# Sums of the dispatch weights by one product with a stationary of ones and a wide reciprocal, in an attention and soft-MoE kernel

## The reference

```python
x = layernorm(x, norm_g, norm_b)                       # B, 512, 256
logits = einsum('bnd,esd->bnes', x, se)                # 512 tokens x 1024 slots an image
dispatch = softmax(logits, axis=1)                     # over the tokens
combine = softmax(logits.reshape(B, N, -1), axis=-1)   # over the slots
slots = einsum('bnd,bnes->besd', x, dispatch)          # weighted sums of the tokens
```

## Time and profile before

| | us |
|---|---|
| median of 3 runs | 1199.85 (1196.84 to 1200.65) |
| the profiled execution, whole | 1196.4 |
| its span, first to last instruction | 1194.7 |
| TensorE busy | 1140.9 (96%) |
| VectorE, ScalarE, GpSimd busy | 780.1, 662.9, 579.2 |
| mean granted TensorE clock | 0.986 |

### The profile page before, as it was taken

The page is one execution under the profiler, slowest core; times in us unless marked ns, Lnnn a source line. Parts: engine busy times, 40 slices in busy tenths (PEclk is TensorE's granted clock), DMA queues, the critical chain, the costliest instruction groups (busy, mean ns, idle before and its releaser), DMA issues.

```text
span 1194.7 us, 19111 instructions
## 1 busy us (share of the span) xinstructions
PE 1140.9 (96%) x6849; PEld 897.2 (75%) x6882; DVE 780.1 (65%) x1251; ACT 662.9 (55%) x946; POOL 579.2 (48%) x399
## 2 busy tenths in 40 slices
PE   7799999999999999988999999979999999999996
PEld 5566667676666666656788888858888888888885
DVE  6878787979797978766677777644455454523344
ACT  2555466565656565656797777755555555530112
POOL 5555555555555556522666666664444544430000
PEclk9899999999999999999899999999999999999998
DMA  5645544645565454631144335365555445365661
GB/s 152 143 106 130 123 115 103 159 113 152 125 155 131 115 157 92 180 98 54 40 160 161 125 125 186 108 195 185 166 183 184 140 157 165 114 216 166 244 224 53
DMA packets 126670, 170.29 MB, mean 143 GB/s; under 512 B 47041, under 2 KB 77186, under 8 KB 126594
## 3 DMA queue, kind: packets, MB, share of 16 engines
q1 hardware_dynamic: 124018, 167.95, 48.2%
q10 hardware_dynamic: 2576, 1.35, 0.5%
HBM read 72.26 MB, written 37.75 MB: 92 GB/s over the span
## 4 chain that ended last, share of the span: by engine, by line
PE 79%; ACT 8%; DVE 6%; issue 3%; POOL 1%; ACTq 1%; DMA 1%; SPq 1%; another core or an unknown queue 0%; DVEq 0%; POOLq 0%
PE ring L455 11%; PE ring L456 11%; PE ring L457 11%; PE ring L1626 7%; PE tail L1487 6%; PE ring L1476 5%; PE ring L1460 4%; PE tail L455 4%; PE tail L456 4%; PE tail L457 4%; ACT pt L873 2%; PE ring L1509 2%; PE tail L1626 2%; PE ring L1563 2%; ACT x L892 2%
## 5 line engine op out<-in xcount | busy, mean ns | idle before, releaser
L1170 DVE TENSOR_REDUCE mx<-ring 128x4 f32<-128x512 f32 (+2 forms) x192 | 199.4, 1041 | 71.9 <-PE ring L1463 54.3
L873 ACT ACTIVATE pt<-ring 128x1024 f32<-128x1024 f32 (+1 forms) x192 | 167.4, 882 | 87.3 <-PE ring L1476 87.1
L723 POOL TENSOR_SCALAR_AFFINE_SELECT pt<-pt 128x512 f32<-128x512 f32 x128 | 81.7, 638 | 192.9 <-ACT pt L873 192.9
L1476 PE MATMUL ring<-qks 98*128 98x256 f32 (+3 forms) x512 | 136.7, 370 | 3.9 <-DVE mx L1170 1.9
L1460 PE MATMUL ring<-qks 96*128 96x384 f32 (+3 forms) x512 | 118.7, 334 | 9.0 <-DMA qks<-stg 3.5
L740 POOL TENSOR_TENSOR dl<-e,dh 128x1024 fp32r<-128x1024 f32 x32 | 76.5, 2404 | 93.4 <-ACT e L944 93.4
L764 POOL TENSOR_TENSOR hl<-hid,hh 128x512 fp32r<-128x512 f32 x64 | 82.7, 1302 | 77.1 <-ACT hh L979 77.1
L817 ACT ACTIVATE lat<-ring,blat 128x512 f32<-128x512 f32 x64 | 40.6, 685 | 128.3 <-PE ring L457 117.4
L1476 PEld LDWEIGHTS ring<-qks 98*128 98x128 f32 x512 | 79.0, 190 | 37.0 <-issue 20.1
L1288 DVE SCALAR_TENSOR_TENSOR hid<-ring,bias_e,gate 128x512 f32<-128x512 f32 x64 | 47.8, 747 | 80.9 <-ACT gate L973 47.0
L1460 PEld LDWEIGHTS ring<-qks 96*128 96x128 f32 x512 | 78.5, 192 | 29.5 <-ACT pt L873 18.8
(11 more groups left out here) (246 smaller groups left out, 3050.9 us busy)
## 6 DMA issues: line engine op xcount, KB each, us to landing
qks<-stg SPq DMA_DIRECT2D x378, 128.0 KB, 2.4
c_dram<-c2s SPq DMA_DIRECT2D x32, 512.0 KB, 5.0
c<-c_dram SPq DMA_DIRECT2D x32, 512.0 KB, 6.2
sl_dram<-sls SPq DMA_DIRECT2D x32, 256.0 KB, 3.4
wg<-in_wg SPq DMA_DIRECT2D x16, 512.0 KB, 5.3
wu<-in_wu SPq DMA_DIRECT2D x16, 512.0 KB, 6.0
wd<-in_wd SPq DMA_DIRECT2D x16, 512.0 KB, 6.9
sl<-sl_dram SPq DMA_DIRECT2D x16, 512.0 KB, 4.5
```

Of the source, the lines that this page charges most:

```text
L723: nc.gpsimd.affine_select(out=m, in_=m, compare_op=ALU.is_ge, fill=0.0, base=0, pattern=[[0, GH], [1, P]], channel_multiplier=-1).then_inc ...
L873: nc.scalar.activation(pt[j][:, h:h + heads, 0:n], heads_of(tile, heads, n), ACT.Exp, scale=SCALE).then_inc(empty, 1)
L1170: nc.vector.tensor_reduce(out=mx[:, g, h:h + heads, i], in_=heads_of(tile, heads, (i + 1) * P), axis=AX.X, op=ALU.max).then_inc(empty, 1)
L1476: last = nc.tensor.matmul(scores[:, h, :], qks[0:KS_ROWS + 2, g, 1, h0 + h, j * P:(j + 1) * P], qks[0:KS_ROWS + 2, g, 0, h0 + h, j * P:T], ...
```

## The change

The two steps `sumT` and `sumB` of a half become one, `sumB`, at the place of `sumT` in the lists of TensorE and VectorE. TensorE makes one f32 product with a stationary operand of 128x128 ones (a column of ones, broadcast) and the 512 columns of partial sums: each partition gets all 512 sums. VectorE takes the reciprocal of 128x512 out of PSUM straight to `sls[h][:, 1, :]`. The transposes, the small reduction and reciprocal, and ScalarE's copy are gone, with their buffers; a period has 15 fills. The column of ones is one more memset on GpSimd and 32 bytes among the constants, so all later arrays lie 32 bytes further; the counts of the start's semaphore move by one.

```diff
 PE_FRONT = (
-    ("sumT", -1, 1), ("topT", 0), ("c2", 0, 0), ("zT", 1), ("c2", 0, 1), ("topB", 0), ("sumB", -1, 1), ("slots", -1, 1), ("s1", 1, 0),
-    ("c2", 0, 2), ("c2", 0, 3), ("s1", 1, 1), ("sumT", 0, 0), ("s1", 1, 2), ("s1", 1, 3), ("sumB", 0, 0), ("slots", 0, 0),
+    ("sumB", -1, 1), ("topT", 0), ("c2", 0, 0), ("zT", 1), ("c2", 0, 1), ("topB", 0), ("slots", -1, 1), ("s1", 1, 0),
+    ("c2", 0, 2), ("c2", 0, 3), ("s1", 1, 1), ("sumB", 0, 0), ("s1", 1, 2), ("s1", 1, 3), ("slots", 0, 0),
 )
 DVE_FRONT = (
-    ("sumT", -1, 1), ("topT", 0), ("zT", 1), ("sub", 0, 0), ("sub", 0, 1), ("xn", 1), ("sub", 0, 2), ("sub", 0, 3), ("slots", -1, 1),
-    ("s1", 1, 0), ("s1", 1, 1), ("sumT", 0, 0), ("s1", 1, 2), ("s1", 1, 3), ("rows", 1), ("slots", 0, 0),
+    ("sumB", -1, 1), ("topT", 0), ("zT", 1), ("sub", 0, 0), ("sub", 0, 1), ("xn", 1), ("sub", 0, 2), ("sub", 0, 3), ("slots", -1, 1),
+    ("s1", 1, 0), ("s1", 1, 1), ("sumB", 0, 0), ("s1", 1, 2), ("s1", 1, 3), ("rows", 1), ("slots", 0, 0),
 )
 PE_LAST = (
-    ("topT", 0), ("c2", 0, 0), ("sumT", -1, 1), ("topB", 0), ("sumB", -1, 1), ("slots", -1, 1), ("c2", 0, 1), ("slots", 0, 0),
-    ("sumT", 0, 0), ("sumB", 0, 0), ("c2", 0, 2), ("c2", 0, 3), ("slots", 0, 1), ("sumT", 0, 1), ("sumB", 0, 1),
+    ("topT", 0), ("c2", 0, 0), ("sumB", -1, 1), ("topB", 0), ("slots", -1, 1), ("c2", 0, 1), ("slots", 0, 0),
+    ("sumB", 0, 0), ("c2", 0, 2), ("c2", 0, 3), ("slots", 0, 1), ("sumB", 0, 1), 
 )
...
+    one = place("one", [P, 1], f32)
...
+            nc.gpsimd.memset(one[:, :], 1.0).then_inc(pool_ready, 1)
...
-                elif name == "sumT":
-                    n = slice(st[2] * 4, st[2] * 4 + 4)
+                elif name == "sumB":
+                    h = st[2]
                     dve.wait_ge(full, fill_count(st))
-                    blink(nc.vector.tensor_reduce(out=es[:, n], in_=tile[:, 0, :].rearrange("p (j q) -> p j q", q=P), axis=AX.X, op=ALU.add))
-                    nc.vector.reciprocal(res[:, n], es[:, n]).then_inc(empty, 1)
+                    dve.wait_ge(sl_stored[h], b * NC * 16)
+                    if b == 0:
+                        read = ("cproj", B - 1)
+                        dve.wait_ge(pair_filled[slot(read)], fill_count(read))
+                    nc.vector.reciprocal(sls[h][:, 1, :], tile[:, 0, :]).then_inc(empty, 1)
...
-                elif name == "sumT":
+                elif name == "sumB":
                     h = st[2]
                     pe.wait_ge(summed, 4 * b + 2 * h + 2)
-                    for j in range(4):
-                        last = nc.tensor.transpose(tile[:, 0, j * P:(j + 1) * P], e2[2 * h][:, 0, j * P:(j + 1) * P], ident[:, :])
-                    last.then_inc(full, 1)
-                elif name == "sumB":
-                    h = st[2]
-                    src = ("sumT", b, h)
-                    pe.wait_ge(pair_drained[slot(src)], fill_count(src))
-                    for j in range(4):
-                        last = nc.tensor.transpose(tile[:, 0, j * P:(j + 1) * P], bcast(res[:, 4 * h + j:4 * h + j + 1], [P, P]), ident[:, :])
-                    last.then_inc(full, 1)
+                    nc.tensor.matmul(tile[:, 0, :], bcast(one[:, 0:1], [P, P]), e2[2 * h][:, 0, :], start=True, stop=True).then_inc(full, 1)
```

More of the change, by code:

```diff
@@ L114 @@
 PE_FRONT = (
-    ("sumT", -1, 1), ("topT", 0), ("c2", 0, 0), ("zT", 1), ("c2", 0, 1), ("topB", 0), ("sumB", -1, 1), ("slots", -1, 1), ("s1", 1, 0),
-    ("c2", 0, 2), ("c2", 0, 3), ("s1", 1, 1), ("sumT", 0, 0), ("s1", 1, 2), ("s1", 1, 3), ("sumB", 0, 0), ("slots", 0, 0),
+    ("sumB", -1, 1), ("topT", 0), ("c2", 0, 0), ("zT", 1), ("c2", 0, 1), ("topB", 0), ("slots", -1, 1), ("s1", 1, 0),
+    ("c2", 0, 2), ("c2", 0, 3), ("s1", 1, 1), ("sumB", 0, 0), ("s1", 1, 2), ("s1", 1, 3), ("slots", 0, 0),
 )
 ACT_FRONT = (
-    ("c2", 0, 0), ("c2", 0, 1), ("xn", 1), ("e", 0, 0), ("e", 0, 1), ("sumB", -1, 1), ("zh", 1), ("e", 0, 2), ("c2", 0, 2), ("s1", 1, 0),
-    ("c2", 0, 3), ("e", 0, 3), ("s1", 1, 1), ("s1", 1, 2), ("s1", 1, 3), ("sumB", 0, 0),
+    ("c2", 0, 0), ("c2", 0, 1), ("xn", 1), ("e", 0, 0), ("e", 0, 1), ("zh", 1), ("e", 0, 2), ("c2", 0, 2), ("s1", 1, 0),
+    ("c2", 0, 3), ("e", 0, 3), ("s1", 1, 1), ("s1", 1, 2), ("s1", 1, 3),
 )
 DVE_FRONT = (
-    ("sumT", -1, 1), ("topT", 0), ("zT", 1), ("sub", 0, 0), ("sub", 0, 1), ("xn", 1), ("sub", 0, 2), ("sub", 0, 3), ("slots", -1, 1),
-    ("s1", 1, 0), ("s1", 1, 1), ("sumT", 0, 0), ("s1", 1, 2), ("s1", 1, 3), ("rows", 1), ("slots", 0, 0),
+    ("sumB", -1, 1), ("topT", 0), ("zT", 1), ("sub", 0, 0), ("sub", 0, 1), ("xn", 1), ("sub", 0, 2), ("sub", 0, 3), ("slots", -1, 1),
+    ("s1", 1, 0), ("s1", 1, 1), ("sumB", 0, 0), ("s1", 1, 2), ("s1", 1, 3), ("rows", 1), ("slots", 0, 0),
 )
@@ L131 @@
 PE_LAST = (
-    ("topT", 0), ("c2", 0, 0), ("sumT", -1, 1), ("topB", 0), ("sumB", -1, 1), ("slots", -1, 1), ("c2", 0, 1), ("slots", 0, 0),
-    ("sumT", 0, 0), ("sumB", 0, 0), ("c2", 0, 2), ("c2", 0, 3), ("slots", 0, 1), ("sumT", 0, 1), ("sumB", 0, 1),
+    ("topT", 0), ("c2", 0, 0), ("sumB", -1, 1), ("topB", 0), ("slots", -1, 1), ("c2", 0, 1), ("slots", 0, 0),
+    ("sumB", 0, 0), ("c2", 0, 2), ("c2", 0, 3), ("slots", 0, 1), ("sumB", 0, 1),
 )
 ACT_LAST = (
-    ("c2", 0, 0), ("e", 0, 0), ("e", 0, 1), ("sumB", -1, 1), ("e", 0, 2), ("c2", 0, 1), ("e", 0, 3), ("weight", 0, 1), ("sumB", 0, 0),
-    ("weight", 0, 2), ("c2", 0, 2), ("weight", 0, 3), ("c2", 0, 3), ("sumB", 0, 1), ("weight", 0, 0),
+    ("c2", 0, 0), ("e", 0, 0), ("e", 0, 1), ("e", 0, 2), ("c2", 0, 1), ("e", 0, 3), ("weight", 0, 1),
+    ("weight", 0, 2), ("c2", 0, 2), ("weight", 0, 3), ("c2", 0, 3), ("weight", 0, 0),
 )
 DVE_LAST = (
-    ("topT", 0), ("sumT", -1, 1), ("sub", 0, 0), ("sub", 0, 1), ("sub", 0, 2), ("sub", 0, 3), ("slots", -1, 1), ("sumT", 0, 0),
-    ("slots", 0, 0), ("weight", 0, 1), ("weight", 0, 3), ("sumT", 0, 1), ("slots", 0, 1), ("weight", 0, 0),
+    ("topT", 0), ("sumB", -1, 1), ("sub", 0, 0), ("sub", 0, 1), ("sub", 0, 2), ("sub", 0, 3), ("slots", -1, 1), ("sumB", 0, 0),
+    ("slots", 0, 0), ("weight", 0, 1), ("weight", 0, 3), ("sumB", 0, 1), ("slots", 0, 1), ("weight", 0, 0),
 )
@@ L153 @@
 POOL_JOIN = ()
-PAIR_STEPS = ("lat", "max", "exp", "v", "yTT", "cproj", "wv", "seT", "zT", "s1", "topT", "topB", "sumT", "sumB", "c2", "slots")
+PAIR_STEPS = ("lat", "max", "exp", "v", "yTT", "cproj", "wv", "seT", "zT", "s1", "topT", "topB", "sumB", "c2", "slots")
 MISC_STEPS = ("wqk", "neg", "yT")
@@ L247, in block_kernel @@
     m2 = place("m2", [P, NS], f32)
-    es = place("es", [P, NS], f32)
-    res = place("res", [P, NS], f32)
     identb = place("identb", [P, P], bf16)
@@ L427, in block_kernel @@
     SE_DVE = WV_DVE + 2 + 3 * NEWTON + 1
-    MASK_READY, POOL_SETUP = 8, 10
+    MASK_READY, POOL_SETUP = 9, 11
     IN_LAT, IN_SMALL, IN_ROPE, IN_SG, IN_SE, IN_TAIL = 5, 7, 2, 3, 1, 4
     ATTN_CHAIN, COMBINE_CHAIN = G + G + 3 + 1 + 3 * NEWTON, 13
-    CHAIN = B * ATTN_CHAIN + B * 2
+    CHAIN = B * ATTN_CHAIN
     cos2, sin2 = (bcast(t[:, :].unsqueeze(1), [P, 2, T]) for t in (cos, sin))
@@ L669, in _ @@
             nc.gpsimd.memset(zeros[:, :, :], 0.0).then_inc(pool_ready, 1)
-            pool.wait_ge(pool_ready, 5)
+            nc.gpsimd.memset(one[:, :], 1.0).then_inc(pool_ready, 1)
+            pool.wait_ge(pool_ready, 6)
             for m in (ident, identb):
@@ L679, in _ @@
             nc.gpsimd.memset(va[:, :, :, HD:L], 1.0).then_inc(pool_ready, 1)
-            pool.wait_ge(pool_ready, 9)
+            pool.wait_ge(pool_ready, MASK_READY + 1)
             nc.gpsimd.memset(fp(qks[KS_ROWS:KS_ROWS + 2, :, 1, :, :]), 1.0).then_inc(pool_ready, 1)
@@ L1257, in _ @@
                     elif u % 2 == 0:
-                        read = ("sumT", b - 1, h)
+                        read = ("sumB", b - 1, h)
                         dve.wait_ge(pair_filled[slot(read)], fill_count(read))
```

2 lines of the change are left out of this document (removed).

## The result

| | before | after |
|---|---|---|
| median | 1198.34 us (4 runs) | 1226.23 us (4 runs, 1225.87 to 1230.95) |
| profiled execution, whole / span | 1196.4 / 1194.7 us | 1225.87 / 1224.1 us |
| mean granted TensorE clock | 0.986 | 0.977 |
| first front sum to first expert product (TensorE starts) | 804.14 - 578.98 = 225.2 us | 833.19 - 578.16 = 255.0 us |

The changed kernel takes 1.0236 times as long (95% interval 1.0218 to 1.0255), 28 us more. The last row holds all of it: the front has become 29.9 us longer, what lies before and after it has moved by less than 1 us.

The account below looks back on a forecast made before the run. TensorE's gapless queue of products bounds the periods, a chain of waits the end; 12.7 us over six periods plus 3.3 in the last image make 16.0 on the shown median 1199.85, so 1216 us, range 1205 to 1233.

Parts of the forecast that it names:

- The loop: Six front periods: two wide reciprocals on the chain between VectorE, ScalarE and TensorE, 29.77 to 31.9 us each, 12.7 in all.
- clock rival: New TensorE stops in each period lower its granted clock: 14.4 us more over six periods, 1230 us; chance 0.12.
- R: Time one wide reciprocal holds VectorE: forecast 3.03 us, 2.1 more than the reduction and small reciprocal it replaces.
- 25.84 + 2R: Front period's length, summed as 12.16 + 13.68 + 2R: 31.9 us forecast, against 29.77 before.
- The reciprocal's length: VectorE's reciprocal over 128x512 out of PSUM: 158 ns plus 512 elements at 5.75 ns, 3.10 us.
- this case's end: Upper end of the forecast case: reciprocal at 6.3 ns an element, R 3.3 us, sum 20.5 us, up to 1220.
- The last image: End of the front, where waits are exposed: reciprocals on the chain to the expert stage add 3.3 us.
- a sign that it was wrong: TensorE's granted clock below 1.00 between 590 and 780 us would show the forecast wrong.
- My stop of 1.6 us: TensorE stands still 1.6 us each period before c2 1, whose PSUM pair the reciprocal frees at 17.0 us.
- TensorE: no gain: Each of 16 sums swaps eight transposes, 0.87 us, for one f32 product, 0.86 us: nothing gained.
- the 32 bytes: Arrays behind the constants move by 32 bytes: taken at nothing, no row bearing on it.
- The fast divide: Rival: wide reciprocal at the copies' rate, R 0.62 us, 3.7 us gained in the last image, 1196; chance 0.12.

Follow-up runs that it names:

- e4_fill: Changed kernel with unused bf16 products filling TensorE's new stops (8 before c2 1, 15 and 12 before the last slots steps): ratio 1.0196 to before.
- e8_fill_apply: Changed kernel with TensorE's new stops filled by unused products and ScalarE's last apply step back at its old place: ratio 1.0156 to before.
- e10_copy_apply: Changed kernel with a copy for the wide reciprocal (division left out) and ScalarE's last apply step back at its old place: ratio 0.9974 to before.
- e3_apply: Changed kernel with ScalarE's last apply step, which had slid later in its list, back where the kernel before had it: ratio 1.0262 to before.
- e1_copy: Changed kernel with a 128x512 copy in place of the wide reciprocal, division left out: ratio 1.0001 to before.
- e7_pad: Kernel before with only the changed kernel's extra memset and 32 bytes among the constants: ratio 1.0000 to before.
- e2_half: Changed kernel with the reciprocal over 256 of 512 columns and a copy of the other 256: ratio 1.0079 to before.
- e11_lnexp2: Changed kernel's product, inverse by ScalarE's logarithm and exponential, logarithm alone freeing PSUM, sumB (b, 0) between s1 1 and s1 2 on ScalarE: ratio 0.9991 to before.

## Why the prediction was right, and where it was off

It said slower, by 16 us, by way of a loop; it is slower by 28, inside the range but nearer to its upper end. The loop is what the runs show; that the range held is in part luck, since of the 12 us beyond the forecast most come from a clock rival given 0.12 and from a step that the forecast did not have. The runs take the front's 29.9 us apart:

| step | front | part |
|---|---|---|
| changed kernel to e4_fill: clock held | 255.0 to 247.4 | 7.6 |
| e4_fill to e8_fill_apply: moved step put back | 247.4 to 244.7 | 2.7 |
| e8_fill_apply to e10_copy_apply: reciprocal to copy, stops gone | 244.7 to 223.0 | 21.7 |
| e10_copy_apply to before: all else that the change does | 223.0 to 225.2 | -2.1 |

The first two steps are one edit each, the third is two. The parts depend on the order in which they are taken: put back by itself, the moved step changed nothing (e3_apply, 255.1), as the clock fell once more. And e10_copy_apply has a fall of the clock of its own in the last image.

- **The loop** was right in every link: the stop before c2 1, topT behind the reciprocal, the drain of slots turned from TensorE's wait to ScalarE's, two reciprocals a period. With the measured reciprocal (R = 3.28 us; the next starts 717.33 - 714.07 = 3.26 after it) the formula 25.84 + 2R gives 32.4; with the clock held it was 32.25.
- **The reciprocal's length** is the term of the sum that was mis-sized: 3.10 forecast, 3.35 measured. The line through 4 and 16 elements had 5.75 ns an element, the slope from 256 to 512 is 6.25. With twelve reciprocals in the periods and four on the last image's chain, 0.25 us more is 4 us: 16 would have been 20. It was under the 6.3 ns that I gave as this case's end, whose 20.5 us it comes to.
- **The last image**: forecast 3.3 us over before. From the seventh front sum to the experts it took 46.53 before, 54.10 after, 51.2 in e8_fill_apply: 4.6 with the clock held, where 37.7 + 4R gives 50.8, or 4.3; 2.9 more by the clock.
- **The clock** was a rival with 0.12, and one or two falls were in the forecast. It fell in four of six periods and at both slots steps of the last image: 7.6 us, against the rival's 14.4 for six. The prediction named a clock below 1.00 between 590 and 780 us as a sign that it was wrong, and the clock was 0.96 from 590 to 770: by that sign the forecast alone fails, and what was measured is the loop of the forecast with about half of the rival's price on top. My stop of 1.6 us was 2.0 to 2.2, because each tenth on R is two tenths on the stop (10.97 + 2R against a fixed 15.4).
- **What the forecast missed outright** is the moved step: 2.7 us with the clock held, 4.8 in e1_copy with a fall of the clock, nothing to be seen in e3_apply. I had written out what the edited lists do to each step of the sums and not what the shorter list does to steps that are inserted by position.
- **TensorE: no gain** was right: e1_copy and e10_copy_apply have periods of 29.68 with one product for eight transposes, against 29.77. So was the small change in PSUM fills and, by e7_pad, the 32 bytes.
- **The fast divide**, the rival on the other side, would have given 1196; e10_copy_apply, which has a copy's time in its place, gave 0.9974 of before, 3 us less: the price was about right, the condition wasn't met. With the moved step left as the change has it, even that gain is absent (e1_copy, 1.0001).

The Trainium skill's "VectorE: DVE Perf Modes", section "First, the fixed hardware budget", has the repeat count of 8 for the reciprocal. The trace agrees that it is far from one step an element, and not with eight: 6.25 ns over a copy's 1.04 (684 ns for 512 elements in e10_copy_apply, 418 for 256 in e2_half) is six.

## What to carry to other kernels

A saving on the engine that sets the pace counts only if what replaces it elsewhere fits the order: here TensorE's queue lost 0.87 and gained 0.86 us, and VectorE, with 8.8 us idle a period, could not take 2.4 us more twice because both stood on the chain from one step's PSUM pair to the next. A wide reciprocal is not a copy; make the inverse on few elements and broadcast it, as the kernel before did, or put it where its engine waits, which gave back two thirds here. After removing entries from an order written by position, compare the whole lists before and after, not the edited entries alone.

## What the runs showed of the hardware that I had not expected

- VectorE's f32 reciprocal: 178 ns for 4 elements a partition, 246 for 16, 1748 for 256, 3350 for 512; a copy of 256 takes 418. ScalarE's logarithm and exponential of 512 elements take 0.60 and 0.63 us, with no load of function tables between them (e11_lnexp2 has two loads in all, as the changed kernel has), so its way to an inverse is 2.7 times shorter.
- An f32 product of one column isn't cheap: eight records for four products, with a weight load each, take 0.8 us and lengthen a period with two such sets by 0.87; four f32 transposes of 128 columns take 0.44.
- Stops of TensorE of 2.0 to 2.2 us were followed by the lower clock in four cases of the changed kernel and not in the one that ends at 696.83. The length of the stop alone does not tell: at the same place in the order, 1.87 us (e10_copy_apply) was followed by it and 1.88 (e1_copy) was not, 2.95 (e1_copy) was and 3.10 (e4_fill) was not. bf16 products to a bank that nobody reads kept the clock at 1.00 from 590 to 800 us and gave back 7.6 us.
